# Moving the float16 copies of four kept samples to GpSimd, and reordering VectorE's work in the steps without y

## The reference, cut to what matters

```python
# x: (32, 256, 56, 56); M = 56*56 = 3136; channels as two halves of 128
im = relu(x), per channel minus its mean mn
p  = clip(u.T @ im, -cv, cv)
q  = round((p - dmin) * scale)          # 8 bits per channel, over all 32 samples
p  = u @ (q / scale + dmin);  p = p - mean(p) + mn
# second layer, per sample
z  = relu(bn(w_conv1 @ p))              # "h" in the kernel
d  = relu(bn(w_dr @ z + b_dr))          # 128 channels, "g" in the kernel
cov = (d - mean(d)) @ (d - mean(d)).T / M
r  = einsum('cjh,bch->bcj', w_row, bn(cov)) + b_row
att = sigmoid(w_fc @ r + b_fc)
out = p * att                           # "y" is p, scaled by att at the end
```

## Time and profile before

| | before |
|---|---|
| median of 3 runs | 1868.07 us (1865.79 to 1869.73) |
| profiled execution | 1868.28 us, span 1866.5 us |
| mean granted TensorE clock | 0.954 |
| TensorE busy | 1695.2 us, 91% |
| VectorE busy | 1576.0 us, 84% |
| ScalarE busy | 1475.6 us, 79% |
| GpSimd busy | 460.2 us, 25%, all in the first stage |

### The profile page before, as it was taken

How to read it: one execution, slowest core, us unless ns; L and a number is a source line. 1 busy time by engine, 2 the same in 40 slices (tenths; PEclk the granted TensorE clock), 3 DMA queues, 4 the chain that set the end, 5 groups by cost and what they waited for, 6 DMA issues and landing times.

```text
span 1866.5 us, 40162 instructions
## 1 busy us (share of the span) xinstructions
PE 1695.2 (91%) x13394; PEld 1317.1 (71%) x13394; DVE 1576.0 (84%) x2897; ACT 1475.6 (79%) x2244; POOL 460.2 (25%) x136
## 2 busy tenths in 40 slices
PE   8999999999993235588899999999999999999999
PEld 8999999999992011366566666666666766666665
DVE  6888888888887788689988888888888888888886
ACT  7777777777778997788778878788788787888886
POOL 7888888888880000000000000000000000000000
PEclk9999999999996567699999999999999999999999
DMA  9998998998999999405546546455465464554535
GB/s 333 375 375 305 375 370 305 378 365 313 373 353 388 430 430 429 194 2 201 191 156 235 169 167 227 157 201 193 165 221 175 163 233 162 189 204 166 213 139 208
DMA packets 141135, 477.37 MB, mean 256 GB/s; under 512 B 10656, under 2 KB 33568, under 8 KB 126368
## 3 DMA queue, kind: packets, MB, share of 16 engines
q1 hardware_dynamic: 141088, 476.75, 69.2%
HBM read 284.04 MB, written 192.68 MB: 255 GB/s over the span
## 4 chain that ended last, share of the span: by engine, by line
PE 51%; DVE 4%; ACT 0%; issue 0%; DVEq 0%; ACTq 0%
PE y_ps L1014 16%; PE z_ps L1040 16%; PE d_ps L965 13%; PE cov_ps L947 5%; DVE hl L1181 1%; DVE gg L1203 1%; PE ch_ps L1025 1%; DVE g L1193 0%; DVE p_res L1274 0%; DVE qr L1149 0%; PE ch_ps L978 0%; PE ch_ps L977 0%; DVE q L1156 0%; PE y_ps L994 0%; PE cov_ps L950 0%
## 5 line engine op out<-in xcount | busy, mean ns | idle before, releaser
L299 POOL TENSOR_TENSOR xl<-early,xh 128x1568 fp32r<-128x1568 f32 x128 | 459.3, 3589 | 97.1 <-ACT xh L258 97.1
L1040 PE MATMUL z_ps<-qr,wl 128*128 128x512 f16 (+2 forms) x896 | 314.5, 354 | 0.0
L1040 PE MATMUL z_ps<-qr,wh 128*128 128x512 f16 (+2 forms) x896 | 314.2, 354 | 0.0
L1181 DVE TENSOR_TENSOR hl<-h,hh 128x1024 f16<-128x1024 f32 (+2 forms) x224 | 243.9, 1089 | 74.5 <-ACT hh L1097 74.3
L258 ACT ACTIVATE xh<-early 128x1568 fp32r<-128x1568 f32 x128 | 194.1, 1517 | 139.8 <-PE pp L316 139.7
L965 PE MATMUL d_ps<-vh,hh 128*128 128x128 f16 x1600 | 280.1, 219 | 7.5 <-DVE hl L1181 7.5
L1092 ACT ACTIVATE h<-z_ps,sb_h 128x512 f32<-128x512 f32 (+2 forms) x448 | 264.0, 625 | 23.6 <-PE z_ps L1040 20.5
L965 PE MATMUL d_ps<-vl,hh 128*128 128x128 f16 x1600 | 279.9, 219 | 0.0
L965 PE MATMUL d_ps<-vh,hl 128*128 128x128 f16 x1600 | 279.9, 219 | 0.0
L316 PE MATMUL pp<-xh,uh 128*128 128x392 f32 x1024 | 267.4, 342 | 9.1 <-ACT xh L258 9.1
L1014 PE MATMUL y_ps<-qr,udh 128*128 128x512 f16 (+2 forms) x784 | 274.1, 353 | 0.0
(11 more groups left out here) (198 smaller groups left out, 2999.7 us busy)
## 6 DMA issues: line engine op xcount, KB each, us to landing
early<-in_x_dram SPq DMA_DIRECT2D x128, 784.0 KB, 6.9
out_dram<-p_res SPq DMA_DIRECT2D x30, 3136.0 KB, 10.2
early<-p_scratch SPq DMA_DIRECT2D x42, 1568.0 KB, 12.7
p_res<-p_scratch SPq DMA_DIRECT2D x112, 512.0 KB, 4.4
p_scratch<-early SPq DMA_DIRECT2D x56, 784.0 KB, 7.8
p_scratch<-late SPq DMA_DIRECT2D x56, 784.0 KB, 7.8
p_res<-p_scratch SPq DMA_DIRECT2D x56, 384.0 KB, 3.2
late_tile<-p_scratch SPq DMA_DIRECT2D x13, 1568.0 KB, 12.8
```

Source lines behind the costliest of these rows:

```text
L299: nc.gpsimd.tensor_tensor(xl[:, k % 2], xs[:, k], xh[:, k % 2].bitcast(F32), ALU.subtract).then_inc(split_done, 1)
L1040: last = nc.tensor.matmul(z_ps[:, m, 0:w], part[:, k, m * P:(m + 1) * P], qr[:, a, k, columns(s)], start=k == 0 and part is wh, stop=k == ...
L1181: nc.vector.tensor_tensor(hl[:, par, :, 0:w], h32[:, par, :, 0:w], hh[:, par, :, 0:w], ALU.subtract).then_inc(h_split, 1)
```

## The change

It does four things. (1) The copies of q to float16 for the four kept samples, 28 chunks, are made by GpSimd in a list of its own: 14 without a wait, then one behind each z that frees its place. VectorE keeps those for samples from DRAM, and waits once, in step 26, for all 28. (2) In the steps without y, VectorE takes the low half of g first, then (if there is one) the copy, then g and the low half of h, and the sums behind them. (3) In steps 1 to 3 of a sample, ScalarE scales both halves of a kept output chunk and VectorE none; `made_scaled` counts accordingly. (4) Y_PLACES has four slots in each of the last three of its pairs, where pair 11 had three; so the work for chunks 18 to 20 of y comes one slot earlier.

```diff
-            (i, t) for i in range(2 * RES + 1, PAIRS - 1) for t in range(3 + (i % 2 == 0))]
+            (i, t) for i in range(2 * RES + 1, PAIRS - 1) for t in range(3 + (i >= PAIRS - 4))]
...
+            def vector_scales(s):
+                return not 1 <= s <= 3
...
+            def scaled_by_vector(chunks):
+                return sum(vector_scales((c + Y_LAG) % CH) for c in range(chunks))
...
-                        sp.wait_ge(made_scaled, CH * n + end)
+                        sp.wait_ge(made_scaled, scaled_by_vector(CH * n + end))
...
+            @block.gpsimd
+            def _(pool):
+                assert MADE >= RES - 2
+                for n in range(RES):
+                    for c in range(CH):
+                        if n >= 2:
+                            pool.wait_ge(z_done, K * (CH * (n - 2) + c + 1))
+                        nc.gpsimd.tensor_scalar(qr[:, n % 2, :, columns(c)], q_kept(ORDER[n])[:, :, columns(c)], HALF,
+                                                None, ALU.subtract).then_inc(q_converted, 1)
...
-                                act.wait_ge(made_scaled, CH * (n - 1))
+                                act.wait_ge(made_scaled, scaled_by_vector(CH * (n - 1)))
...
-                                kept = kept_y(o, c)[:, 0]
-                                nc.scalar.activation(kept, kept, ACT.Identity, scale=att_cy[:, 0, 0:1],
-                                                     bias=att_cy[:, 0, 1:2]).then_inc(y_free, K)
+                                own = 1 if vector_scales(s) else K
+                                for m in range(own):
+                                    kept = kept_y(o, c)[:, m]
+                                    last = nc.scalar.activation(kept, kept, ACT.Identity, scale=att_cy[:, m, 0:1],
+                                                                bias=att_cy[:, m, 1:2])
+                                last.then_inc(y_free, K)
...
-                for c in range(LEAD):
-                    convert(0, c, q_kept(ORDER[0])[:, :, columns(c)])
...
-                        if s == 1:
+                        if s == 1 or has_no_y(r2, a, s):
                             low_half_of_g(r2, a, s)
-                        if has(r2, a, s, -LEAD):
+                        if has(r2, a, s, -LEAD) and from_dram(r2, a, s):
                             n, c = converted_chunk(r2, a, s)
-                            if from_dram(r2, a, s):
-                                part = quantise(n, c)
+                            part = quantise(n, c)
+                            if isinstance(r2, int) and n == RES and c == 0:
+                                dve.wait_ge(q_converted, CH * RES)
+                            if made(g + LEAD - 2 * CH):
+                                dve.wait_ge(z_done, K * (g + LEAD - 2 * CH + 1))
                             else:
-                                part = q_kept(ORDER[n])[:, :, columns(c)]
-                            if has(r2, a, s, 2 * CH - LEAD):
-
-                                if made(g + LEAD - 2 * CH):
-                                    dve.wait_ge(z_done, K * (g + LEAD - 2 * CH + 1))
-                                else:
-                                    dve.wait_ge(y_done, K * (g + LEAD - (2 + MADE) * CH + 1))
+                                dve.wait_ge(y_done, K * (g + LEAD - (2 + MADE) * CH + 1))
                             convert(a if s + LEAD < CH else 1 - a, c, part)
-                        if s != 1:
+                        if not (s == 1 or has_no_y(r2, a, s)):
                             low_half_of_g(r2, a, s)
...
+                        if not has_no_y(r2, a, s):
+                            sums_of_covariance(r2, a, s)
                         if has_no_y(r2, a, s):
                             rectified_g(r2, a, s)
                             low_half_of_h(r2, a, s)
-                            if has(r2, a, s, CH + Y_LAG):
+                            sums_of_covariance(r2, a, s)
+                            if has(r2, a, s, CH + Y_LAG) and vector_scales(s):
```

More of the change, by code:

```diff
@@ L1204, in low_half_of_g, with sums_of_covariance @@
                                                 gg[0:dq, par, 0:dt, 0:P], ALU.subtract).then_inc(g_split, 1)
+                def sums_of_covariance(r2, a, s):
+                    n = 2 * r2 + a
+                    if s == 1 and exists(r2, a, back=1):
+                        dve.wait_ge(cov_done, first_chunk(r2, a))
+                        nc.vector.tensor_copy(hl_sb[:], cov_ps[:, P:2 * P]).then_inc(hl_copied, 1)
+                        nc.vector.tensor_scalar(dg[:], ident[:], cov_ps[:, 2 * P:2 * P + 1], -1.0 / M, ALU.mult,
+                                                ALU.mult).then_inc(diag_done, 1)
+                        nc.vector.tensor_copy(s_sb[:], cov_ps[:, 2 * P:2 * P + 1])
+                        dve.wait_ge(hl_copied, n)
+                        nc.vector.tensor_tensor(a_sb[:], cov_ps[:, 0:P], hl_sb[:], ALU.add).then_inc(cov_read, 1)
+                    if s == 2 and exists(r2, a, back=1):
+                        dve.wait_ge(spread_done, n)
+                        dve.wait_ge(cov_read, n)
+                        nc.vector.scalar_tensor_tensor(out=a_sb[:], in0=ch_ps[:, P:2 * P], scalar=s_sb[:, 0:1],
+                                                       in1=a_sb[:], op0=ALU.mult,
+                                                       op1=ALU.add).then_inc(cov_centred, 1)
+                        dve.wait_ge(cov_centred, 2 * n - 1)
+                        nc.vector.tensor_tensor(cov_sb[:], ch_ps[:, 0:P], a_sb[:],
+                                                ALU.add).then_inc(cov_centred, 1)
+                        dve.wait_ge(cov_centred, 2 * n)
+                        for j in range(J):
+                            last = nc.vector.scalar_tensor_tensor(
+                                out=prod[:, j], in0=wr[:, j], scalar=1.0, in1=cov_sb[:], op0=ALU.mult,
+                                op1=ALU.mult, accum_out=r0[:, j:j + 1])
+                        last.then_inc(r_summed, 1)
+                        dve.wait_ge(r_summed, n)
+                        nc.vector.tensor_tensor(r[:], r0[:], rconst[:], ALU.add).then_inc(r_done, 1)
+                    if s == 3 and exists(r2, a, back=1):
+                        dve.wait_ge(r_done, n)
+                        wait_from(dve, logits_done, n - 1)
+                        nc.vector.tensor_scalar(weighted[:], wfc_t[:, 0], r[:, 0:1], None,
+                                                ALU.mult).then_inc(weighted_done, 1)
+                        for j in range(1, J):
+                            dve.wait_ge(weighted_done, J * (n - 1) + j)
+                            nc.vector.scalar_tensor_tensor(
+                                out=weighted[:], in0=wfc_t[:, j], scalar=r[:, j:j + 1], in1=weighted[:],
+                                op0=ALU.mult, op1=ALU.add).then_inc(weighted_done, 1)
@@ L1206, in phase @@
                 def phase(r2, a):
-                    n = 2 * r2 + a
                     for s in range(CH):
```

## The result

The changed kernel took 1880.2 us, median of 6 runs (1876.15 to 1880.73), against 1867.98 us for the kernel before (6 runs, 1865.79 to 1869.73): a ratio of 1.0058, interval 1.0048 to 1.0067. It is 12 us slower, where I had forecast 10 us faster. The profiled execution has a span of 1878.4 us and a mean granted clock of 0.945.

A forecast was written before the change was run, and what follows sets the result against it. Steps without y were taken as bound by VectorE, except sample 0 by TensorE. Gains of 0.5, 2.8, 2.0, 2.3 and 2.7 us in samples 0 to 4, together 10.3, gave 1858 us; range 1853 to 1863, 8 in 10 to 1874.

The forecast's parts named there:

- rival 1: Steps without y: VectorE instructions with two SBUF inputs wait until GpSimd's copy ends; 1870 us, chance 0.30.
- Both signs that I had named for a failure: Steps without y: a copy costing over 2 us, or VectorE's own instructions stretching beside it.
- ScalarE's scalings: Steps 1 to 3 of a sample: three scalings move; VectorE loses 1.38 us a sample, ScalarE gains 1.7.
- The gain from the copies' absence: Steps without y: 28 copies leave VectorE's path, 4.35 us in sample 2.
- the first copy is there at 774.8: Start of third stage: GpSimd's first copy takes 1.67 us, ready before TensorE reads at 775.28.
- my upper bound of 2.38 us: GpSimd's copy of 1024 elements, bounded above by its float32 subtraction of two tensors, 2.23 ns per element.
- its upper price: GpSimd's copies at 2.1 us on average, with exclusion of VectorE: step of 5.7 us, 15 us lost, 1883 us.
- The wait for weighted: Logits of step 4 in a sample without y: TensorE stands 1.9 us until weighted ends.
- The gain of sums last: Sample 4: last sums, behind hl in step 3, mostly run under the first y; 1.5 us gained.
- At nothing: Last pairs of second stage: slot added to Y_PLACES counted as no change, up to 1.3 us if DMAs don't cover it.
- Sample 0: First sample of the third stage: bound by TensorE, only 0.5 us gained.

The follow-up runs named there:

- spare copies: Kernel before with 28 copies added on GpSimd into a tile nobody reads, VectorE still making its own: 1.0046, 1877.44 us.
- only weighted first: Changed kernel with only the sums of step 3 back ahead of g and the low half of h, copies on GpSimd: 1.0029, 1873.82 us.
- weighted first with VectorE's copies: Changed kernel with copies on VectorE, weighted ahead of g and the low half of h, sums of steps 1 and 2 last: 1.0013, 1872.0 us.

## Why the prediction was wrong

Two steps failed. The sum took the copies off VectorE as pure gain and put what GpSimd does to VectorE's own instructions at nothing, leaving it to rival 1: they stretch by 11.6 us in all, and copies on GpSimd cost 0.22% to 0.50% instead of gaining. And it counted late sums as a gain, with a stand of 1.9 us as their only price: they cost 0.31% with the copies on VectorE and 0.59% with them on GpSimd. Both signs that I had named for a failure came, a copy above 2 us and stretched instructions of VectorE.

| | copies on VectorE | copies on GpSimd |
|---|---|---|
| sums first | 0.9977 | 0.9999 |
| sums last | 1.0008 | 1.0058 |

All four have ScalarE's scalings, gg first and the new slots. The gain from these is 0.23%, GpSimd costs 0.22% where the sums come first, late sums 0.31% where VectorE copies, and the two together 0.28% more than their sum: 0.9977 + 0.0022 + 0.0031 + 0.0028 = 1.0058. The last term has an error of about 0.18. For it the traces offer a reason that I didn't test by itself. Sample 1 takes 28.1 and 28.3 us with the copies on VectorE, 30.2 with them on GpSimd and the sums first, and 34.9 with both changes: 4.5 us more than the two one by one, nearly all of the term. There, with GpSimd at work, the last three instructions of weighted take 1.96 us instead of 1.52, the stand before the logits grows to 2.35 us, and the clock falls for some 7 us. The other three falls of the changed kernel (four in all, against once, twice and once in the other three kernels of the table) come when GpSimd has finished, and cost little: its samples 2 and 3 are within 0.2 us of those of the kernel with the copies on VectorE and the sums last. Each is seen in one execution only.

By the steps of the prediction:

- **The gain from the copies' absence** was a term too large, since the price stood beside it as a rival at 0.30. The step "the first copy is there at 774.8", with 1.54 ns per element from the select, failed in size: 2.77 us for 1024 elements, 2.7 ns each, above my upper bound of 2.38 us. A difference of two float32 tensors was no upper bound for a conversion from bytes. At the start it shows by itself: the first z comes 2.92 us after the first copy begins in all five kernels with GpSimd's copies, and 1.87 us in the kernel before, so 1.05 of the 2.3 us by which the first h is later here.
- **Rival 1 was right in kind.** VectorE's hl, gg, prod and weighted do wait, and p_res too. Its working was wrong twice, in opposite senses: the copies are longer than I took them for, and a wait ends after 0.9 us at most, not with the copy. That its upper price gave 1883 us, near the 1880 measured, is luck, since it has no loss from late sums in it. Beside a VectorE that makes its own copies too, GpSimd's copies cost 8.6 us (spare copies, 0.46%); in place of them, 0.22% with the sums first.
- **The wait for weighted** I had at 1.9 us; it measured 2.35, 1.72, 1.72 and, in sample 4, 1.18. The length was right, and the price wrong: I charged the wait and not the half clock after it. In the ten windows with a low clock some 8.6 us of full-clock time is missing ((1 - clock) x 3 us, summed), not all of it on the path.
- **The gain of sums last** was a guess with the wrong sign. In sample 4 I took 1.5 us for it, because the last sums would run under y. Steps 28 to 31 did get shorter by 0.8 us (2.7 forecast, scalings included), and steps 32 to 34 longer by 1.5. Ahead of the low half of h, the sums delay hl, and TensorE waits up to 1.2 us for it; behind it, they delay gg, g and weighted, and TensorE waits longer and in one piece. Each of the three other places tried for them lost 0.30 to 0.36% against sums first (last place with GpSimd's copies: 0.59%).
- **ScalarE's scalings** were right in sign: 0.17%, 3.2 us, against 4.1 us of VectorE's time moved in samples 2 to 4; some 2 us of it can be placed in the traces.
- **At nothing**: the new slot. The third stage starts between 773 and 776 us in all runs with and without it; the later start here (774.7 against 773.1) can't be told from how executions differ, and the slot was not tested by itself.
- **Sample 0** (0.5 us forecast) took 0.2 us more: TensorE is busy 25.40 of 26.20 us there, so VectorE's stretched instructions cost little. But it took 23.4 us in the two profiled executions in which the clock had risen before 780 us. GpSimd's waits show in sample 1.

Open stays what share of the 12 us each low-clock stretch has: no run here could hold the clock while leaving the stand. Open too is how far the late sums bring the falls about.

## What to carry to other kernels

Before work is moved to GpSimd, count it against the VectorE instructions beside it: here 0.69 us taken away from VectorE cost 2.8 us of GpSimd and up to 0.9 us of waiting in each of 20 VectorE instructions. Count a long stand of TensorE at more than its length, for it may run at half clock behind it, though it does not every time. Change one thing at a time: of four edits that went in together, one was worth 0.17%, one (the slot) could not be told from nothing, and two lost more than the first gained. The low half of g first, which went in with the second, was within error.

## What was unexpected of the hardware

GpSimd's subtraction of a number from bytes into float16 takes 2.7 ns per element and partition at 1024 elements, more than its float32 subtraction of two tensors (2.29 ns per element). A VectorE instruction in conflict with it waits 0.9 us at most, not the 2.8 us of the copy, and the profile counts the wait as busy time. After stands of TensorE of 1.7 to 2.7 us its granted clock fell to the lower level in some cases and not in others: three stands of 2.00 us in one execution were followed by one fall, and one kernel (only weighted first) had stands of 1.73, 2.06 and 1.77 us without any. The clearest case is the wait of 1.77 us for gg in sample 4, which the changed kernel and ten of the twelve others have alike: within 1.5 us behind it the clock fell in five of the eleven. In three others of the profiled executions (sums first with GpSimd's copies, spare copies, weighted first with VectorE's copies) a fall came with no wait above 1.13 us just ahead. So the length of the last stand alone does not tell whether the clock falls.
